# Scaling the gathered expert rows on the vector engine instead of the activation engine

## The reference, cut to what matters

```python
x = x + L0_attn(layernorm(x))     # chunked gated linear attention, 16 heads
x = x + L0_ffn(layernorm(x))      # a shared expert and the best of 8 routed experts
x = x + L1_attn(layernorm(x))     # projection, convolution, scan, output product
x = x + L1_ffn(layernorm(x))      # fp4-quantised gate, up and down products
```

```python
scores = x @ router                                  # 4096 x 8
gate   = sigmoid(score of the best expert), 0 for the other seven
row    = gate * x                                    # the scaling of this document
mid    = silu(row @ w1[e]) * (row @ w3[e])           # width 352
routed = mid @ w2[e]
```

## Time and profile before

| | |
|---|---|
| median of 3 executions | 633.02 us |
| the three executions | 633.72, 631.06, 633.02 us |
| the profiled execution | 633.72 us, its span 631.9 us |
| mean granted clock of PE | 0.952 of full speed |
| busy over the span | PE 551.3 us (87%), DVE 449.9 (71%), ACT 317.7 (50%), POOL 350.0 (55%) |
| phase C | from about 286.6 to 391 us of the span |

### The profile page before, as it was taken

One profiled execution on the slowest core, in us unless ns is written; L12 is line 12 of the kernel. 1 busy time (PEld: TensorE's weight loads), 2 busy tenths in 40 slices (PEclk: granted clock), 3 DMA queues, 4 the chain that ended last, 5 costly groups with the idle time before them and its releaser, 6 DMA issues. The chain is left out here.

```text
span 631.9 us, 15237 instructions
## 1 busy us (share of the span) xinstructions
PE 551.3 (87%) x4532; PEld 451.9 (72%) x4533; DVE 449.9 (71%) x1175; ACT 317.7 (50%) x902; POOL 350.0 (55%) x519
## 2 busy tenths in 40 slices
PE   2699999999999997997799997378999999999966
PEld 1466676777776685877699996357887887788755
DVE  2789999999985569643934342147999998999873
ACT  1456666666675542334446553144555456555532
POOL 4578777777775315376833300843777567664131
PEclk9999999999999999997979999598999999999975
DMA  7000011011011430115122201211111101110000
GB/s 207 17 29 34 28 39 39 25 41 33 25 50 53 124 101 25 49 26 133 40 55 57 59 25 34 25 14 13 18 18 22 29 17 17 26 23 10 8 18 17
DMA packets 35320, 25.60 MB, mean 41 GB/s; under 512 B 4752, under 2 KB 31696, under 8 KB 35280
## 3 DMA queue, kind: packets, MB, share of 16 engines
q1 hardware_dynamic: 29392, 20.39, 10.8%
q0 software_dynamic: 5888, 4.72, 4.8%
HBM read 14.09 MB, written 6.82 MB: 33 GB/s over the span
## 5 line engine op out<-in xcount | busy, mean ns | idle before, releaser
L1097 PE MATMUL a_ps_a<-a_qx,a_kt 32*128 32x512 f32 x512 | 67.3, 613 | 1.3 <-DMA a_qx<-a_qs 1.3
L193 POOL DMA_INDIRECT rows<-xn_dram,slot_token x40 | 40.4, 1009 | 40.4 <-ACT c_rows L1403 24.8
L1618 POOL DMA_INDIRECT x<-yg_dram,pos x32 | 56.1, 1753 | 11.8 <-issue 11.8
L1260 POOL TENSOR_TENSOR d_hq<-d_fh_v,d_fh_scale 128x352 f32<-128x352 f32 x32 | 27.9, 888 | 61.3 <-DVE d_fh_v L1286 61.3
L436 POOL TENSOR_SCALAR_AFFINE_SELECT a_at<-a_at 128x512 f32<-128x512 f32 x80 | 50.5, 650 | 12.8 <-ACT a_at L525 12.8
L1442 DVE TENSOR_TENSOR c_hid<-c_act,c_ps 128x352 f32<-128x352 f32 x40 | 20.5, 519 | 42.8 <-ACT c_act L1389 42.8
L525 ACT ACTIVATE a_at<-a_ps_a 128x512 f32<-128x512 f32 x80 | 44.5, 600 | 9.8 <-PE a_ps_a L1097 8.2
L1097 PEld LDWEIGHTS a_ps_a<-a_qx,a_kt 32*128 32x128 f32 x512 | 31.3, 184 | 16.6 <-issue 15.9
L201 PE MATMUL d_ps_A<-d_xnT,wmix 128*128 128x256 f32 x128 | 38.4, 300 | 1.6 <-DVE d_xnT L1797 0.9
L1389 ACT ACTIVATE c_act<-c_ps 128x352 f32<-128x352 f32 x40 | 18.5, 463 | 40.8 <-PE c_ps L203 40.8
L202 PE MATMUL d_ps_A<-d_xnT,wmix 128*128 128x256 f32 x128 | 37.2, 290 | 0.0
(11 more groups left out here) (287 smaller groups left out, 1804.0 us busy)
## 6 DMA issues: line engine op xcount, KB each, us to landing
a_qx<-a_qs SPq DMA_DIRECT2D x64, 64.0 KB, 1.9
a_at<-in_L_ffn_w_eDF_dram SPq DMA_DIRECT2D x16, 176.0 KB, 3.0
yg_dram<-c_y SPq DMA_DIRECT2D x20, 128.0 KB, 2.0
xn_dram<-a_xn2s SPq DMA_DIRECT2D x16, 128.0 KB, 1.9
out_dram<-x SPq DMA_DIRECT2D x16, 128.0 KB, 1.8
w<-in_L_ffn_w_eFD_dram SPq DMA_DIRECT2D x2, 512.0 KB, 5.2
x<-in_L_attn_x_dram SPq DMA_DIRECT2D x1, 768.0 KB, 5.3
rows<-xn_dram,slot_token POOLq DMA_INDIRECT x40, 2.7
```

Of the source, the lines that this page charges most:

```text
L193: nc.gpsimd.indirect_dma_start(out=g["rows"][:, k % 4, t, :], out_offset=None, in_=g["xn2_dram"][:, :], in_offset=bass.IndirectOffsetOnAxi ...
L1097: last = nc.tensor.matmul(ps_a[:, r, :, :], kt[rows, b.par, c_, tile(t)], qx[rows, b.par, :, c_, tile(t)], start=(c_ == 0), stop=(c_ == 1))
L1618: nc.gpsimd.indirect_dma_start(out=x[:, t, :], out_offset=None, in_=g["yg_dram"][:, :], in_offset=bass.IndirectOffsetOnAxis(ap=g["pos"][:, ...
```

## The change

The scaling leaves ACT's body and enters DVE's, where it stands behind the two `c_hid` and ahead of `prepare`. It still handles pair j+2 in body j and has the same waits. ACT's bodies become a loop, DVE's are all written out, now beginning with body -2.

```diff
@@ scalar, body(j)
                     nc.scalar.activation(xT[:, k.par, 0, :, :], ps_t[:, 0:2, :], ACT.Copy).then_inc(s_xT, 1)
-                if live(j + 2):
-                    k = j + 2
-                    act.wait_ge(g["s_rows"][k.off % 4], 32 * (k.off // 4 + 1))
-                    done(act, s_xp, k, ago=2)
-                    for t in range(2):
-                        c0 = 2 * k.off + t
-                        last = nc.scalar.activation(rows[:, k.par, t, :], g["rows"][:, k.off % 4, t, :], ACT.Identity,
-                                                    scale=g["slot_gate"][:, c0:c0 + 1])
-                    last.then_inc(s_rg, 1)
                 if live(j):
                     first_product(j, 0)
...
-            for j in range(-2, LAST + 1):
-                body(Seq(j))
+            run_skewed(act, body, -1, LO, HI, LAST)
@@ vector, body(j)
                         nc.vector.tensor_tensor(hid[:, j.par, t, :], act1[:, t, :], ps_3[:, t, 0:F], ALU.mult).then_inc(s_h, 1)
+                if live(j + 2):
+                    k = j + 2
+                    dve.wait_ge(g["s_rows"][k.off % 4], 32 * (k.off // 4 + 1))
+                    done(dve, s_xp, k, ago=2)
+                    for t in range(2):
+                        c0 = 2 * k.off + t
+                        last = nc.vector.tensor_scalar(rows[:, k.par, t, :], g["rows"][:, k.off % 4, t, :],
+                                                       g["slot_gate"][:, c0:c0 + 1], None, ALU.mult)
+                    last.then_inc(s_rg, 1)
                 if 1 <= j.off < LO:
                     for n in range(3 * j.off - 3, 3 * j.off):
                         prepare(n)
...
-            run_skewed(dve, body, -1, LO, HI, LAST)
+            for j in range(-2, LAST + 1):
+                body(Seq(j))
```

## The result

The changed kernel takes 660.49 us (median of four executions, 659.28 to 662.65) against 632.04 us for the kernel before: a ratio of 1.0457 (95% interval 1.0409 to 1.0505), 28.5 us slower. The forecast was 659.0, the range 653 to 668. Its profiled execution took 662.3 us, with a span of 660.6.

A forecast was written before the change was run, and what follows sets the result against it. PE was taken to bound phase C's regular part and to wait for DVE's scaling after the change: 1.6 (pair 2) + 2.6 (pairs 3 to 6) + 21.1 (pairs 7 to 19) = 25.3 us on 633.72, so 659; range 653 to 668.

The forecast's parts named there:

- The chain at a boundary: Regular part of phase C: transposes wait for scaling behind c_hid, 1.62 us a boundary, pair 6.13 instead of 4.51 us.
- The scaling's duration: DVE scaling in phase C: 281 ns as for L693, a pair of scalings in 0.46 us.
- Rival 1: The DVE scaling is short, 229 ns, a pair in 0.36 us: 1.8 us less, 657.2 in all; chance 25%.
- Start and pair 2: Start of phase C: pairs 0 and 1 together cost 0; pair 2's transposes wait 1.6 us.
- Pairs 3 to 6: Bodies 1 to 3 with prepare, DVE the bound: scalings add 1.2 us, the wait ahead of pair 6 1.4; together 2.6.
- Rival 3: Bodies 1 to 3: POOL and DVE block each other and it falls on the scaling, 5.8 us: 665; chance 8%.
- The clock: Full clock in phase C's regular part, nothing added; longer pause ahead of pair 6 may lengthen its slow stretch by up to 3 us.
- rival 2: Clock falls in the regular part too: 3.4 us more for each of 13 pairs, 703, or 674; chance 7%.
- The sum: Whole kernel: 1.6 + 2.6 + 21.1 = 25.3 us added to the profiled 633.72, giving 659.0.
- Rival 4: Not slower: scaled rows are ready by 350.25, so PE is not held; 633.5; chance 3%.

The follow-up runs named there:

- second pair of traces: Changed kernel and kernel before, each executed and traced once more, nothing altered: 660.57 us, ratio 1.0419, and 632.17 us; phase C 130.2 and 101.2 us.
- spread version: Against the kernel before: scaling on DVE ahead of c_hid, the nine prepare instructions one in each of bodies 1 to 9; ratio 0.9914, again 0.9922.
- doubled kernel: Changed kernel with two more DVE scalings per body into a spare tile, ahead of the real two: 673.6 us, ratio 1.0587 to the kernel before.
- first experiment: Changed kernel with only DVE's scaling moved ahead of the two c_hid: 638.41 us against 636.0 for the kernel before, ratio 1.0004.

## Why the prediction was right, step by step

- **The chain at a boundary**: forecast 1.62 us, PE waits 1.50 and 1.58. Right, and shown from four sides: earlier place, later deadline, other engine, doubled member. The pair takes 6.32, not 6.13: of 1.81 us, 1.62 were seen. The missing 0.19 lies in terms that I took over from a PE that never stopped. By the rows above, `c_hid` to scaling is 0.44 (0.42 forecast), the pair of scalings 0.48 (0.46), its hand-over 0.05 and 0.13 by turns (0.04), and behind the pause `down` follows the transposes by 0.28 and 0.32 where it was 0.22. These give 0.04 + 0.05 + 0.08 = 0.17; `down` to `up` adds up to 0.04 (1.60 and 1.66 against 1.59): all of the 0.19, as far as the rows are exact. The kernel with ACT's late scaling shows the same 0.05 and 0.13, 0.28 and 0.32, 1.60 and 1.66, with DVE looped and ACT written out, so these terms come with the stall and not with the new loop forms. Over 12 intervals 21.7 us against 19.4.
- **The scaling's duration**: 281 ns, the value of L693 to the nanosecond. Rival 1 with its 229 ns falls. The skill's rule (the Trainium skill, VectorE: DVE Perf Modes, section "The perf-mode tier table (the rule you actually need)") did not bring the short time; the 199 ns of L1278 on 70 elements, with constants as factors, lie on the slope that agrees with it. Whether the rule fails for this form or something fixed is added is not shown: the form was run at 128 elements alone, and the column need not be the reason, since the DVE copy L691 of this shape, without a factor (but with its elements reordered), takes 278 ns in the kernel before.
- **Start and pair 2**: the first wait is 1.74 instead of 1.78 and pair 1 waits 1.32 instead of 1.05, nothing won; pair 2 waits 1.50 (1.6 forecast).
- **Pairs 3 to 6**: forecast 4.2 up to pair 6 with pair 2, measured 3.4 and 5.8. In the first trace the parts differ from mine. I had DVE bound there and its scalings added to the queue. But `prepare` became shorter, since POOL's long instructions fell beside other instructions: in both traces of the kernel before L1278 takes 2.05 or 2.15 us beside POOL's L1373, in both of the change POOL starts L1373 behind it. Two instructions of it in the kernel after (busy us, mean ns | idle before), then one in the kernel before:

```profile
L1285 DVE SCALAR_TENSOR_TENSOR c_w_sum<-c_w_k,c_w_v 128x1120 f32<-128x1120 f32 x1 | 1.3, 1317 | 0.0
...
L1278 DVE TENSOR_SCALAR c_w_scale<-c_w_amax 128x70 f32<-128x70 f32 x1 | 0.2, 199 | 0.0
```
```profile
L1285 DVE SCALAR_TENSOR_TENSOR c_w_sum<-c_w_k,c_w_v 128x1120 f32<-128x1120 f32 x1 | 3.5, 3526 | 0.0
```

  L1278 took 2050 ns before, and L1282 went from 2807 to 1312. The nine together went from 14.4 to 8.9 us. PE's stalls at each boundary had given DVE time as well, and every wait of the transposes is now one for the scaled rows. The 5.8 of the second pair of traces hold a longer stretch at the lower clock (below).
- **Rival 3** has the right mechanism and the wrong size. One pair of scalings of the change was held, by 0.6 us (323.64, 1.05 instead of 0.48, beside POOL's L1380 from 321.11 to 324.41). How it looks when it hits fully is seen in the timeline of the kernel that scales one pair ahead:

```profile
311.88 2.92 POOL L1380 TENSOR_TENSOR wmix<-c_wtap,wmix 128x1280 fp32r<-128x1280 f32 x1
312.48 2.61 DVE L1439 TENSOR_SCALAR c_rows<-rows,slot_gate 128x128 f32<-128x128 f32 x2
```

  DVE's pair ends at 315.09, 0.3 us behind POOL's product. That the later of the two waits for the other's whole instruction is what the Trainium skill (SBUF — State Buffer, section Who interferes with whom) states; these rows agree, and the kernel as a whole, at 1.0022, was not measurably slower. In the second trace of the spread version PE did wait for scalings that were held so (0.50 and 0.63 us).
- **The clock**: in the regular part at 1.00 with PE 73% busy; rival 2 falls for this kernel. It came once in the doubled kernel, whose pauses are 0.4 us longer (0.51 in 376.5 to 380.0). On the slow stretch I had the wrong sign: I expected the pause ahead of pair 6 to grow and its slow stretch to last longer. The pause shrank, 2.08 us against 2.68, and no slow stretch followed (6.44 us to pair 7 in both traces of the change). Nor does the pause decide by its length alone, as the prediction read from one trace: in the second trace of the kernel before it is 2.68 us as well, and the clock stays at 1.00 behind it. Instead the stretch at the start of the phase varied: it reached further in the second trace of the change (7.59 us from pair 2 to 3 against 5.27 in the first). These are differences of 2 us between executions of one kernel.
- **The sum** was 25.3 us. Measured 28.5 by the medians, interval 25.8 to 31.9, and 26.8 by the four traces of phase C. The mechanism was right; the mis-sized term is the boundary, 1.81 instead of 1.62, with 2.3 us over 12 intervals. That 659.0 came within 1.5 us of 660.49 is in part luck: it was added to the profiled 633.72, and the median of the kernel before came out at 632.04, which hid 1.7 of the 3.2 us that the sum was short. The start and the slow stretches also differed from their terms, by amounts that changed between executions.
- **Rival 4** would have needed the scaling ahead of `c_hid`; the first experiment is that kernel, at 1.0004.

Not settled: how ACT's loop form reaches PE. With the early scaling the traces show `down` to `up` 1.63 to 1.69 us long, where it is 1.58 to 1.61 with ACT written out, and no wait that names the cause.

## What to carry to other kernels

When work moves to an idler engine, look first at what stands ahead of it in that engine's queue and whether that depends on the consumer: here a scaling of 0.46 us cost 1.8 us at each regular boundary, as it was queued behind the last result of the very engine that was waiting for its rows. The busy shares (DVE 41%, ACT 59% of the regular part) say that there is room, and only the deadline in each body says where; a place ahead of the two products or a pair further ahead made the same move free in time, to within 0.5%. But a move that is free is not a gain where a third engine sets the pace; the gain lay in a burst of DVE work that could be spread over bodies with room.

## What the runs showed of the hardware

In phase A the first 16 score products (L1097) take 2.00 us in one execution and 3.79 in another. The rows of the kernel after, of the kernel before, and of the second trace of the kernel before:

```profile
27.10 3.79 PE L1097 MATMUL a_ps_a<-a_qx,a_kt 32*128 32x512 f32 x16 [0.97 <-DMA a_qx<-a_qs]
```
```profile
27.14 2.00 PE L1097 MATMUL a_ps_a<-a_qx,a_kt 32*128 32x512 f32 x16 [1.28 <-DMA a_qx<-a_qs]
```
```profile
27.32 3.80 PE L1097 MATMUL a_ps_a<-a_qx,a_kt 32*128 32x512 f32 x16 [0.99 <-DMA a_qx<-a_qs]
```

The busy times of that stretch in the last of these, and of the first 8 us of the kernel after, columns as in the earlier trace rows:

```profile
27.10:30.90 3.80, 3.58 (x16) 1.31 (x16) 1.71 (x3) 0.00 (x0) 2.10 (x5) 0.50 0.00 0
```
```profile
0.00:8.00 8.00, 0.00 (x0) 0.01 (x1) 0.00 (x0) 1.28 (x1) 6.07 (x8) 1.00 0.51 139
```

So 3.80 us is what the lower level of the clock gives, in the one trace that records it there. In the kernel after, the same stretch is listed with 1.00, but that is no reading: its record of the clock begins at 36.6 us, and a stretch ahead of the record is listed with 1.00 even where PE has done nothing, as in 0 to 8. That the 3.79 us are the lower level too is therefore inferred from their length.

In fourteen traces of eleven kernels, whose phase A is the same, the third batch's exponential (L561) starts at 36.6 to 36.9, 38.2 to 38.8 or 40.1 to 40.5 us, three levels that don't go with the kernel: the change has 40.31 and 38.83, the kernel before 36.62 and 38.59. They go with the moment at which the long entry of full clock begins in the record: 25.1 to 25.8 us in the three traces of the first level, 30.3 to 31.8 in the five of the second, 36.0 to 36.7 in the six of the third. Two executions of one program thus differ by 2.0 us, and the first traces of before and after by 3.7, before the first 41 us are over. That fits a clock that rises at another moment each time; no run sets this moment. A single pair of traces is to be compared stage by stage.
